# A gated delta-rule layer on one core: whole-row transfers around the substitution, two z buffers, 48 stationary columns in the 16x16 merges, q's squares added on VectorE, new queue orders

## The chip, the core and the metric

The kernel runs on one core of a Trainium2 chip, everything in float32. The metric is the device time of one launch in microseconds. The core has five engines with their own instruction queues (TensorE, VectorE, ScalarE, GpSimd and SyncE, which here only issues DMAs), and they meet only through semaphores.

## What is computed

x has 16 sequences of 256 tokens and 256 channels. The reference is a gated delta-rule attention between layer norms, then a gated feed-forward layer, each added to x. Cut to what matters here (q, k, v, z come from a projection of the normed x, q, k, v through a causal convolution of four taps over time, 32 heads of 64 columns):

```python
q = _l2norm(q) * DK ** (-0.5)
k = _l2norm(k)
def step(Sstate, xs):
    q_t, k_t, v_t, g_t, b_t = xs
    Sstate = Sstate * jnp.exp(g_t)[..., None, None]
    kv = jnp.einsum('bhk,bhkv->bhv', k_t, Sstate)
    delta = (v_t - kv) * b_t[..., None]
    Sstate = Sstate + k_t[..., :, None] * delta[..., None, :]
    o_t = jnp.einsum('bhk,bhkv->bhv', q_t, Sstate)
    return (Sstate, o_t)
_, o = lax.scan(step, S0, (qs, ks_, vs, gs, bs))
var = jnp.mean(o * o, -1, keepdims=True)
o = o * lax.rsqrt(var + EPS) * norm_weight * jax.nn.sigmoid(z)
return o.reshape(Bsz, Sl, VDIM) @ w_out.T
```

## The kernel before

It has three stages. Stage one norms x, turns it and computes the gates for all tokens (8 blocks of 512 tokens). Stage two is the attention. Stage three is the feed-forward layer. The change is in stage two, with a little at the end of stage one.

**Stage two** has 64 steps: 8 groups of four heads times 8 blocks of 512 tokens (two sequences). All is unrolled. The scan is computed in chunks of C = 64 tokens: a step has G = 16 matrices of 64x64 (2 head pairs, 2 sequences, 4 chunks) on each half of the 128 partitions, since two heads share the partitions.

A step passes these stations. `project` (L1142) makes eight 128x512 products of the weights and x: k (0, 1), q (2, 3), v (4, 5), z (6, 7). The taps of the convolution are added: for k and v by VectorE (`conv`, L945), for q by ScalarE (`tap_product`) and GpSimd (`add_tap`). `k_tokens` and `v_tokens` (L1148) turn k and v through a 64x64 identity. `scores` (L1165) makes k'k and q'k, and `matrices` (L992) multiplies them with the decays into `a_mat` (strictly lower triangular once masked) and `p_t`.

Then (1 + A) must be inverted for each chunk. Its four diagonal 16x16 blocks are inverted by forward substitution on VectorE (`substitute`, L958), with 128 blocks side by side, one in each partition. So the blocks travel: `units_out` (L593) writes the diagonal blocks of `a_mat` to `a_d` in DRAM with 8 DMAs, `units_in` reads them with one block per partition, and the inverse goes back two ways: as `x_un` through `x_d` into `x_row`, and turned (`turn_units`) as `t_un` through `z_d` into `z_t` and, its odd blocks, into `z_low`. TensorE then merges pairs of 16x16 blocks (`join16_inner`, `join16_outer`, L1176 to L1192) and pairs of 32x32 blocks (`join_inner`, `join_outer`), with ScalarE copying each product out of bank 5. The scratch tensors hold only the blocks, packed.

Then the chunks run one after the other: `key_state` (old state times k), `residual` (VectorE), `solve` (with z_t), `delta_out` (ScalarE), `advance`, `new_state` (VectorE), `output`. At the end the outputs are normed: var(o) + an epsilon that depends on q's norm. `square_o` squares o into `u_sq`, `square_q` squares q into `q_sq`; `epsilon_q` and `sum_squares` (L1257 to L1261) add both over the 64 rows of a head with two matmuls on the constant matrices `ones[:,1]` and `ones[:,0]` into the same bank. `log_var`, `combine`, `gates`, `gated` follow, then `project_out` and `accumulate` into `acc`.

**The order** is written out by hand. Each engine has a function `turn(s)`, called 67 times; `s[k]` is the step that is k turns old, so one turn carries parts of up to four steps, and every engine executes its list strictly in that order. `wait_for(engine, semaphore, step, ...)` stands ahead of an item that needs another engine's result. SyncE's list (L630) does the same for the DMAs, all on one queue. `mats_done`, `z_in`, `z_low_in`, `x_row_in`, `zt_done`, `rhs_done` are such semaphores.

Four buffers of TensorE's results (banks 0 to 3) are handed round between projections, tokens, scores, squares and output products; bank 4 holds states and solves, bank 5 the merges, banks 6 and 7 the outputs.

## Time and profile before

| | |
|---|---|
| median of 3 runs | 3640.7 us (3633.98 to 3648.48) |
| the profiled execution | 3642.9 us, span 3641.1 us, mean granted TensorE clock 0.974 |
| stage one, two, three | about 0 to 163, 163 to 3251, 3251 to 3641 us |
| busy: TensorE, its weight loads, VectorE, ScalarE, GpSimd | 93%, 63%, 63%, 49%, 30% |
| DMA queue of SyncE | 572208 packets, 267 MB, 27% of 16 engines |

Each float32 matmul shows as two records, with a weight load (PEld) and a matmul (PE) for each. Matmuls are pipelined, so the printed durations of neighbours overlap; the distance between starts is what an item costs in a full queue. "Idle before" an instruction, and who released it, tell whether an engine was waiting. An engine that sits idle while another is full costs nothing.

### The profile page before, as it was taken

To read this page: it belongs to the slowest core of one execution; us is meant where nothing else is said; L and a number is where in the kernel's file an instruction comes from. 1 tells how busy PE (TensorE), PEld (TensorE's weight loads), DVE (VectorE), ACT (ScalarE), POOL (GpSimd) and SP (SyncE) were. 2 spreads that over 40 slices of the span, in tenths; PEclk is the share of its full clock that TensorE was granted. 3 is DMA by queue.
4 is the path that set the end of the run, shared out by engine and by line. 5 is a ranking of instruction groups with operands and counts; after the bars stand their busy time and mean duration, and the time that the engine had idled before them with its cause. 6 is when DMAs were issued, how large, how long until landed. Compare 5 with 4: busy or idle time off the path is not lost. (4 is left out here: it accounts for less than half of the span.)

```text
span 3641.1 us, 118760 instructions
## 1 busy us (share of the span) xinstructions
PE 3372.2 (93%) x51264; PEld 2286.7 (63%) x51264; DVE 2288.9 (63%) x5697; ACT 1788.2 (49%) x3338; POOL 1089.7 (30%) x904
## 2 busy tenths in 40 slices
PE   4489999999999999999999999999999999969998
PEld 2256666666666666666666666666666666645554
DVE  5456666666666666666666666666666666635555
ACT  2245555555555555555555555555555555523333
POOL 1043333333333333333333333333333333300000
PEclk7689999999999999999999999999999999979999
DMA  2233233323333333333332233333332333210000
GB/s 76 65 85 82 82 84 87 83 71 83 85 83 84 87 87 86 86 82 81 85 86 76 77 84 86 85 83 86 87 85 78 84 86 87 63 59 18 23 24 18
DMA packets 572727, 274.83 MB, mean 75 GB/s; under 512 B 475696, under 2 KB 521136, under 8 KB 563888
## 3 DMA queue, kind: packets, MB, share of 16 engines
q1 hardware_dynamic: 572208, 267.25, 27.2%
q8 instruction: 407, 6.67, 0.8%
q14 instruction: 112, 0.92, 0.1%
HBM read 190.02 MB, written 35.13 MB: 62 GB/s over the span
## 5 line engine op out<-in xcount | busy, mean ns | idle before, releaser
L1144 PE MATMUL bank<-xT,w_sb 128*128 128x512 f32 x2048 | 1002.6, 618 | 25.7 <-DMA w_sb<-in_w_qkvz 24.7
L681 POOL TENSOR_TENSOR kq<-kq,products 128x510 f32<-128x510 f32 (+2 forms) x384 | 442.3, 1159 | 892.6 <-ACT products L768 738.4
L1144 PEld LDWEIGHTS bank<-xT,w_sb 128*128 128x128 f32 x2048 | 354.5, 190 | 338.3 <-issue 282.7
L818 ACT COPY delta<-bank 128x256 f32<-128x256 f32 x256 | 95.3, 372 | 639.3 <-PE bank L1227 639.3
L950 DVE SCALAR_TENSOR_TENSOR kq<-bank,cw,kq 128x510 f32<-128x510 f32 (+2 forms) x384 | 285.9, 745 | 101.9 <-ACT kq L762 92.8
L669 POOL TENSOR_TENSOR dec_a<-gcrow,gccol 128x1024 f32<-128x1024 f32 x64 | 121.7, 1901 | 614.0 <-DVE p_t L996 323.5
L950 DVE SCALAR_TENSOR_TENSOR v_c<-bank,cw,v_c 128x510 f32<-128x510 f32 (+2 forms) x384 | 285.8, 744 | 15.2 <-ACT v_c L762 6.2
L1028 DVE TENSOR_TENSOR acc<-acc,bank 128x512 f32<-128x512 f32 x128 | 88.1, 688 | 316.7 <-PE bank L1266 316.7
L1171 PE MATMUL bank<-kq 64*64 64x128 f32 x4096 | 278.5, 275 | 1.7 <-DVE p_t L996 1.7
L1171 PEld LDWEIGHTS bank<-kq 64*64 64x64 f32 x4096 | 217.4, 132 | 76.4 <-issue 71.2
L1266 PE MATMUL bank<-wo,u_sq 128*128 128x256 f32 x1024 | 259.3, 397 | 3.4 <-DVE u_sq L1021 3.4
L768 ACT ACTIVATE products<-bank,cw 128x512 f32<-128x512 f32 x384 | 250.4, 689 | 2.4 <-POOL kq L681 2.4
L1252 PEld LDWEIGHTS bank<-p_t,delta 64*64 64x64 f32 x4096 | 215.1, 136 | 47.8 <-issue 47.8
L1252 PE MATMUL bank<-p_t,delta 64*64 64x64 f32 x4096 | 243.3, 220 | 0.0
L1250 PEld LDWEIGHTS bank<-q_g,state 64*64 64x64 f32 x3072 | 179.6, 134 | 95.5 <-issue 95.5
L968 DVE TENSOR_TENSOR x_un<-x_un,prod_un 128x15 f32<-128x15 f32 (+7 forms) x960 | 200.0, 208 | 32.8
L1266 PEld LDWEIGHTS bank<-wo,u_sq 128*128 128x128 f32 x1024 | 187.1, 192 | 46.8 <-issue 21.3
L964 DVE TENSOR_TENSOR prod_un<-a_un,x_un 128x15 f32<-128x15 f32 (+7 forms) x960 | 196.5, 205 | 26.5
L762 ACT ACTIVATE kq<-bank,cw 128x512 f32<-128x512 f32 x256 | 170.1, 697 | 84.4 <-PE bank L1144 83.2
L1250 PE MATMUL bank<-q_g,state 64*64 64x64 f32 x3072 | 205.9, 226 | 1.1 <-ACT delta L818 1.1
L1227 PE MATMUL bank<-rhs,z_t 64*64 64x64 f32 x3072 | 129.0, 220 | 73.2 <-DVE rhs L1004 73.0
L701 POOL TENSOR_TENSOR dec_a<-dec_a,cols 128x1024 f32<-128x1024 f32 x64 | 121.7, 1901 | 233.0 <-DVE b_eg L990 233.0
(137 smaller groups left out, 6259.7 us busy)
## 6 DMA issues: line engine op xcount, KB each, us to landing
w_sb<-in_w_qkvz SPq DMA_DIRECT2D x64, 1024.0 KB, 6.6
gcrow<-gcrow_d SPq DMA_DIRECT2D x128, 256.0 KB, 4.3
xT<-xT_d SPq DMA_DIRECT2D x64, 512.0 KB, 3.4
k_old<-kq SPq DMA_DIRECT2D x64, 512.0 KB, 3.0
wo<-in_w_out SPq DMA_DIRECT2D x64, 256.0 KB, 6.9
gcrow<-in_x SPq DMA_DIRECT2D x16, 512.0 KB, 3.9
x_un<-eye_un SPq DMA_DIRECT2D x64, 128.0 KB, 2.8
a_d<-a_mat SPq DMA_DIRECT2D x512, 16.0 KB, 1.7
```

Source lines behind the costliest of these rows:

```text
L681: ins = nc.gpsimd.tensor_tensor(t[:, :, d:SEQ], t[:, :, d:SEQ], prod[:, :, 0:SEQ - d], ALU.add)
L762: ins = nc.scalar.activation(dst, bank[:, :], ACT.Identity, scale=cw[:, s * TAPS + TAPS - 1:s * TAPS + TAPS])
L768: ins = nc.scalar.activation(products[i % 4][:, :], bank[:, :], ACT.Identity, scale=cw[:, w:w + 1])
L950: ins = nc.vector.scalar_tensor_tensor(t[:, :, d:SEQ], src[:, :, 0:SEQ - d], cw[:, w:w + 1], t[:, :, d:SEQ], ALU.mult, ALU.add)
L964: own.need(own.mark(nc.vector.tensor_tensor(prod, a_un[:, j + 1:B, j:j + 1].broadcast_to([P, rows, wid]), x_un[:, j:j + 1, 0:wid].broadcas ...
L968: ins = nc.vector.tensor_tensor(rest, rest, prod, ALU.subtract)
L1144: ins = nc.tensor.matmul(bank[:, :], w_sb[:, h, s * P:(s + 1) * P], xT[:, h, :], start=(h == 0), stop=(h == HT - 1))
L1171: ins = nc.tensor.matmul(bank[half, i * P:(i + 1) * P], kq[m.par][half, 0, s // 2, t0:t0 + C], kq[m.par][half, :, s // 2, t0:t0 + C], star ...
L1227: ins = nc.tensor.matmul(banks[4][half, 256 + i * C:256 + (i + 1) * C], z_t[half, g, :], rhs[half, i, :] if c else v_r[m.par][half, g, :], ...
L1250: nc.tensor.matmul(o, state[c % 2][half, i, :], q_g[m.par][half, g, :], start=True, stop=False)
L1252: ins = nc.tensor.matmul(o, delta[half, i, :], p_t[m.par][half, g, :], start=(c == 0), stop=True)
L1266: ins = nc.tensor.matmul(bank[:, t * HID:(t + 1) * HID], u_sq[:, a, (2 * k + t) * P:(2 * k + t + 1) * P], wo[m.par][:, a, :], start=(a == ...
```

## The change

**Layout.** The three scratch tensors become whole 64x64 matrices, each padded by 64 elements, so that a diagonal 16x16 block starts every 16*65 elements. `whole` addresses all rows, `diagonal` only the 16x16 blocks on the diagonal. The zeros off the diagonal of z_d and x_d are written once, at the end of stage one. `z_low` is gone: its blocks are read out of z_t, which has two buffers now. Each transfer is split by partition half: 12 DMAs per step where there were 27.

**The 16x16 merges** load 48 stationary columns instead of 64 (the last 16 rows of the result are not needed) and write 48 rows of bank 5, which is cleared once.

**q's squares** are scaled while they are squared (0.064 squared is 64 x 64 x 1e-6) and added to u's squares on VectorE, so one matmul per half is left.

**The orders** of all five queues are new. TensorE's list is shown whole, of the others the parts around the substitution.

```diff
-        a_d, z_d, x_d = (scratch(n, [UNITS, B, B]) for n in ("a_d", "z_d", "x_d"))
+        a_d, z_d, x_d = (scratch(n, [2, G * MAT]) for n in ("a_d", "z_d", "x_d"))
+        def whole(t, h):
+            return t[h].rearrange("(g x) -> g x", x=MAT)[:, 0:C * C].rearrange("g (i c) -> i g c", c=C)
+        def diagonal(t, h):
+            return t[h].rearrange("(u x) -> u x", x=MAT * B // C)[:, 0:B * C].rearrange("u (i c) -> u i c", c=C)[:, :, 0:B]
...
+                    for h in range(2):
+                        zero = z_t[0][D * h:D * h + D, :, :]
+                        sp.dma_start(whole(z_d, h), zero).then_inc(zeros_out, 16)
+                        sp.dma_start(whole(x_d, h), zero).then_inc(zeros_out, 16)
+                    sp.wait_ge(zeros_out, 64)
...
                     def units_out(m):
                         for h in range(2):
-                            for k in range(4):
-                                u, r = (4 * h + k) * G, D * h + B * k
-                                sp.dma_start(a_d[u:u + G].rearrange("g i j -> i g j"),
-                                             a_mat[m.par][r:r + B, :, B * k:B * k + B]).then_inc(a_d_out, 16)
+                            sp.dma_start(whole(a_d, h), a_mat[m.par][D * h:D * h + D, :, :]) \
+                                .then_inc(a_d_out, 16)
                     def units_in(m):
-                        sp.dma_start(a_un[:, :, :], a_d).then_inc(a_un_in, 16)
+                        for h in range(2):
+                            sp.dma_start(a_un[D * h:D * h + D, :, :], diagonal(a_d, h)) \
+                                .then_inc(a_un_in, 16)
                     def z_out(m):
-                        sp.dma_start(z_d, t_un[:, :, :]).then_inc(z_d_out, 16)
+                        for h in range(2):
+                            sp.dma_start(diagonal(z_d, h), t_un[D * h:D * h + D, :, :]) \
+                                .then_inc(z_d_out, 16)
...
+                            sp.dma_start(z_t[m.par][D * h:D * h + D, :, :], whole(z_d, h)).then_inc(z_in, 16)
...
                     def turn(s):
+                        if s[3]:
+                            identity_in(s[3])
+                        if s[2]:
+                            wait_for(sp, conv_done[5], s[2], 1, back=1)
+                            wait_for(sp, tap_done[5], s[2], 1, back=1)
+                            load_cw(s[2])
+                        if s[3]:
+                            wait_for(sp, mats_done[0], s[3], 1)
+                            units_out(s[3])
                         if s[2]:
                             wait_for(sp, qg_done[1], s[2], 1, back=1)
                             load_gates(s[2])
                         if s[3]:
+                            wait_for(sp, a_d_out, s[3], 32)
                             units_in(s[3])
                             wait_for(sp, zt_done, s[3], 1)
                             z_out(s[3])
+                            load_wo(s[3])
+                            keep_k(s[3])
+                            x_out(s[3])
+                            wait_for(sp, z_d_out, s[3], 32)
+                            z_back(s[3])
+                            wait_for(sp, x_d_out, s[3], 32)
                             x_back(s[3])
+                        if s[1]:
+                            wait_for(sp, proj_full[7], s[1], 1, back=1)
+                            load_xw(s[1])
...
                     def square_q(m):
-                        nc.scalar.activation(q_sq[:, :, :], kq[m.par][:, 1, :, :], ACT.Square)
+                        nc.scalar.activation(q_sq[:, :, :], kq[m.par][:, 1, :, :], ACT.Square, scale=0.064)
...
+                    def add_squares(m, a):
+                        nc.vector.tensor_tensor(u_sq[:, a, :], u_sq[:, a, :], q_sq[:, a, :], ALU.add).then_inc(sq_added[a], 1)
...
                     def join16_inner(m):
-                                ins = nc.tensor.matmul(banks[5][half, g * W2:(g + 1) * W2], a_mat[m.par][half, g, :],
-                                                       z_low[half, g, :], start=True, stop=True)
+                                ins = nc.tensor.matmul(banks[5][D * h:D * h + 3 * B, g * W2:(g + 1) * W2], a_mat[m.par][half, g, 0:3 * B],
+                                                       z_t[m.par][half, g, :].rearrange("p (k e c) -> p e k c", k=2, c=B)[:, 1, :, :], start=True, stop=True)
...
                     def join16_outer(m):
-                                ins = nc.tensor.matmul(banks[5][half, g * W2:(g + 1) * W2], x_row[half, g, :],
+                                ins = nc.tensor.matmul(banks[5][D * h:D * h + 3 * B, g * W2:(g + 1) * W2], x_row[half, g, 0:3 * B],
...
-                    def epsilon_q(m, a, bank):
-                        nc.tensor.matmul(bank[:, :], ones[:, 1, :], q_sq[:, a, :], start=True, stop=False)
-
                     def sum_squares(m, a, bank):
-                        nc.tensor.matmul(bank[:, :], ones[:, 0, :], u_sq[:, a, :], start=False, stop=True).then_inc(ss_full[a], 1)
+                        nc.tensor.matmul(bank[:, :], ones[:, 0, :], u_sq[:, a, :], start=True, stop=True).then_inc(ss_full[a], 1)
```

TensorE's new list for one turn, in words, with the bank and the step's age (1, 2, 3 for s[1], s[2], s[3]; 0 for s[0]), and in brackets what it waits for from VectorE, ScalarE, GpSimd or a DMA:

project 6 (1); output 0 (3); solve 1 (3) [rhs_done 1]; project 2 (1) [conv of k 1]; advance 1 (3) [delta 1]; project 0 (1); output 1 (3); key_state 2 (3) [state 1]; project 3 (1); k_tokens 1 (1) [z_exp 0]; solve 2 (3) [rhs_done 2]; project 4 (1) [tap_done 2]; advance 2 (3) [delta 2]; k_tokens 0 (1) [conv of k 0]; output 2 (3); key_state 3 (3) [state 2]; project 5 (1) [tap_prod 5]; solve 3 (3) [rhs_done 3]; project 7 (1) [kt_done 1]; output 3 (3) [delta 3]; scores 3 (1) [conv 4, tap_added 5]; join16_inner (2) [z_in]; scores 2 (1) [kt_done 0]; scores 1 (1) [conv 5]; join16_outer (2) [p16_done, x_row_in]; scores 0 (1) [z_exp 1]; sum_squares 1 and 0 (3) [sq_added]; join_inner (2) [z16_done]; v_tokens 1 and 0 (1) [mats_done 1, 0]; join_outer (2) [p1_done, xtop_done]; project 1 (0) [comb_done 1, xw_in]; solve 0 (2) [zoff_done]; project_out 1 (3) [og_done]; advance 0 (2) [delta 0]; project_out 0 (3); key_state 1 (2) [k_old_in, state 0].

VectorE's new list: tail (1); substitute columns 2 to 5 (2); new_state 1 (3); substitute columns 6 to 14 (2); residual 2 and decay_state 2 (3); conv 0 (1); new_state 2 (3); sum_k 1, scale_k 1 (1); residual 3 (3); sum_k 0, conv 4, scale_k 0, columns, conv 5, matrices 2 and 3 (1); add_squares 1 and 0 (3); matrices 1 and 0 (1); turn_back (2); combine 1 and 0 (3); scale_v 1 and 0 (1); gated 1 and 0 (3); conv 1 (0); accumulate 1 (3); new_state 0, decay_state 1 (2); accumulate 0 (3); residual 1 (2); substitute columns 0 and 1 (1) [a_un_in, x_un_in].

## Rows read from the trace of the kernel before

**Rows 1.** Busy time by engine, 500 to 3000 us; first line names the columns.
```profile
core 0: us, PE busy (x) PEld busy (x) DVE busy (x) ACT busy (x) POOL busy (x), PEclk, DMA share, GB/s
500.00:3000.00 2500.00, 2420.99 (x41095) 1677.82 (x41095) 1648.60 (x4112) 1337.78 (x2484) 894.38 (x742) 1.00 0.31 84
```
**Rows 2.** TensorE's waits, 500 to 3000 us: total us, times, longest.
```profile
PE bank L1227 <- DVE rhs L1004: 57.2, 54, 1.1
PE bank L1181 <- DMA z_low<-z_d: 11.5, 19, 1.6
PE bank L1144 <- DMA w_sb<-in_w_qkvz: 7.6, 19, 0.7
```
**Rows 3.** Line L1014, the state copy of each step: duration ns, first and last start.
```profile
L1014 DVE COPY state<-bank x64: 424/425/426, 246.0 to 3221.0; 128x256 f32<-128x256 f32 x64
```
**Rows 4.** TensorE's timeline, one turn: start us, duration us, engine, line, operation.
```profile
1500.71 2.06 PE L1181 MATMUL bank<-z_low,a_mat 64*64 64x32 f32 x64
1502.60 2.06 PE L1153 MATMUL bank<-masks,kq 64*64 64x64 f32 x64
1504.49 2.01 PE L1190 MATMUL bank<-p,x_row 64*64 64x32 f32 x64
1506.43 1.98 PE L1144 MATMUL bank<-xT,w_sb 128*128 128x512 f32 x4
1508.34 1.09 PE L1171 MATMUL bank<-kq 64*64 64x128 f32 x16
1509.36 1.20 PE L1199 MATMUL bank<-z_t,a_mat 32*32 32x32 f32 x64
1510.49 1.09 PE L1171 MATMUL bank<-kq 64*64 64x128 f32 x16
...
1526.48 0.63 PE L1227 MATMUL bank<-rhs,z_t 64*64 64x64 f32 x16
1526.94 1.10 PE L1153 MATMUL bank<-masks,v_c 64*64 64x64 f32 x32
...
1533.04 3.70 PE L1144 MATMUL bank<-xT,w_sb 128*128 128x512 f32 x8
1536.67 0.68 PE L1217 MATMUL bank<-state,k_old 64*64 64x64 f32 x16
...
1543.83 1.98 PE L1258 MATMUL bank<-q_sq,ones 128*128 128x512 f32 x4
1545.65 1.88 PE L1261 MATMUL bank<-u_sq,ones 128*128 128x512 f32 x4
1547.46 2.06 PE L1181 MATMUL bank<-z_low,a_mat 64*64 64x32 f32 x64
```
**Rows 5.** DMAs: SyncE's timeline; line L235; issues with KB each, us to landing.
```profile
1519.50 4.17 SPq L597 DMA_DIRECT2D a_d<-a_mat  x8
...
L235 SPq DMA_DIRECT2D gccol_d<-v_r x8: 354/359/367, 38.6 to 157.8; - x8
...
w_sb<-in_w_qkvz SPq DMA_DIRECT2D x64, 1024.0 KB, 6.6
gccol_d<-v_r SPq DMA_DIRECT2D x8, 64.0 KB, 2.1
```
**Rows 6.** Groups of instructions by line: busy us, mean ns, idle before and releaser.
```profile
L950 DVE SCALAR_TENSOR_TENSOR kq<-bank,cw,kq 128x510 f32<-128x510 f32 (+2 forms) x384 | 285.9, 745 | 101.9 <-ACT kq L762 92.8
L968 DVE TENSOR_TENSOR x_un<-x_un,prod_un 128x15 f32<-128x15 f32 (+7 forms) x960 | 200.0, 208 | 32.8
L964 DVE TENSOR_TENSOR prod_un<-a_un,x_un 128x15 f32<-128x15 f32 (+7 forms) x960 | 196.5, 205 | 26.5
L1004 DVE TENSOR_TENSOR rhs<-v_r,rhs 128x256 f32<-128x256 f32 x192 | 119.3, 622 | 6.5
L1021 DVE TENSOR_TENSOR u_sq<-bank,gate 128x512 f32<-128x512 f32 x128 | 87.7, 687 | 80.8 <-ACT gate L829 80.7
L808 ACT COPY p<-bank 32x512 f32<-32x512 f32 x128 | 73.6, 575 | 98.7 <-PE bank L1199 98.0
```

More of the change, by code:

```diff
@@ L44, in gated_delta_sandwich @@
     W2 = 2 * B
-    UNITS = 4 * 2 * G
+    MAT = C * C + C
     TAPS = 4
@@ L95, in gated_delta_sandwich @@
         kt = [sb(f"kt{i}", [P, G, C]) for i in range(2)]
-        z_t = sb("z_t", [P, G, C])
+        z_t = [sb(f"z_t{i}", [P, G, C]) for i in range(2)]
         k_tok = sb("k_tok", [P, G, C])
@@ L116, in gated_delta_sandwich @@
         x_row = sb("x_row", [P, G, C])
-        z_low = sb("z_low", [P, G, W2])
         p16 = sb("p16", [P, G, W2])
@@ L263, in _ @@
                 def _(pool):
-                    nc.gpsimd.memset(z_t[:, :, :], 0.0)
-                    nc.gpsimd.memset(z_low[:, :, :], 0.0)
-                    nc.gpsimd.memset(x_row[:, :, :], 0.0)
+                    nc.gpsimd.memset(z_t[0][:, :, :], 0.0).then_inc(zeros, 1)
                     nc.gpsimd.memset(acc[:, :, :], 0.0)
@@ L1272, in turn @@
                         if s[1]:
-                            wait_for(pe, comb_done[0], s[1], 1, back=2)
-                            project(s[1], 7, banks[0])
-                            wait_for(pe, tap_added[5], s[1], 1)
-                            scores(s[1], 2, banks[1])
+                            wait_for(pe, vr_done[0], s[1], 1, back=1)
+                            project(s[1], 6, banks[0])
+                        if s[3]:
+                            output(s[3], 0)
+                            wait_for(pe, rhs_done[1], s[3], 1)
+                            solve(s[3], 1)
@@ new lines, in turn @@
+                        if s[1]:
+                            wait_for(pe, conv_done[1], s[1], 1)
+                            wait_for(pe, tap_done[1], s[1], 1)
+                            project(s[1], 2, banks[1])
+                        if s[3]:
+                            wait_for(pe, delta_done[1], s[3], 1)
+                            advance(s[3], 1)
+                        if s[1]:
+                            project(s[1], 0, banks[2])
+                        if s[3]:
+                            wait_for(pe, qg_done[1], s[3], 1)
+                            output(s[3], 1)
+                            wait_for(pe, state_done[1], s[3], 1)
+                            key_state(s[3], 2)
@@ new lines, in turn @@
+                        if s[1]:
+                            project(s[1], 3, banks[3])
+                            wait_for(pe, z_exp[0], s[1], 1)
+                            k_tokens(s[1], 1, banks[0])
+                        if s[3]:
+                            wait_for(pe, rhs_done[2], s[3], 1)
+                            solve(s[3], 2)
+                        if s[1]:
+                            wait_for(pe, tap_done[2], s[1], 1)
+                            project(s[1], 4, banks[1])
@@ new lines, in turn @@
+                        if s[3]:
+                            wait_for(pe, delta_done[2], s[3], 1)
+                            advance(s[3], 2)
+                        if s[1]:
+                            wait_for(pe, conv_done[0], s[1], 1)
+                            wait_for(pe, tap_done[0], s[1], 1)
+                            k_tokens(s[1], 0, banks[2])
+                        if s[3]:
+                            output(s[3], 2)
+                            wait_for(pe, state_done[2], s[3], 1)
+                            key_state(s[3], 3)
@@ new lines, in turn @@
+                        if s[1]:
+                            wait_for(pe, tap_prod[5], s[1], 1)
+                            project(s[1], 5, banks[3])
+                        if s[3]:
+                            wait_for(pe, rhs_done[3], s[3], 1)
+                            solve(s[3], 3)
+                        if s[1]:
+                            wait_for(pe, kt_done[1], s[1], 1)
+                            project(s[1], 7, banks[0])
+                        if s[3]:
+                            wait_for(pe, delta_done[3], s[3], 1)
+                            output(s[3], 3)
```

537 lines of the change are left out of this document (224 added, 313 removed).

## Prediction

> **What bounds the kernel now.** I read four views in this order. First the busy time by engine over the middle of the kernel [rows 1]: in 2500 us of the long stage, TensorE is busy for 2421 us (97%) at full granted clock, VectorE for 66%, ScalarE 54%, GpSimd 36%, the DMA engines 31%. So TensorE's queue is the first suspect, but a busy TensorE may hide waits, so next the waits [rows 2]: in the same stretch TensorE waited 57.2 us for `rhs`, 11.5 us for `z_low` and 7.6 us for the projection weights, 76 us in all, and for nothing else worth a number. Third, the pace: the copy that each of the 64 steps makes once [rows 3] starts at 246.0 us and for the last time at 3221.0 us, so 63 turns take 2975 us, 47.22 us each; 2500 us are 52.9 turns, so the waits are 1.44 us of a turn and 45.78 us is TensorE's own work, one instruction behind the other. Fourth, the order of that work in one turn [rows 4], where the distance from one start to the next is what an item costs (the printed durations overlap).
>
> The conclusion: in the long stage (about 3090 of 3641 us) time is the sum of what TensorE executes per turn plus 1.44 us. Removing TensorE work pays in full as long as no other queue comes late.
>
> **The change, part by part (per turn; 63 turns).**
>
> 1. q's squares leave TensorE. Before, two 128x512 matmuls with `ones[:,1]` (four records) stand in one run with the two for u's squares: 1543.83 to 1547.46, 3.63 us for eight records [rows 4]. What stays is four records of that shape alone, which is what a single projection costs: 1506.43 to 1508.34, 1.91 us [rows 4]. Saved: 1.72 us.
>
> 2. The 16x16 merges load 48 stationary columns where they loaded 64. They cost 1.89 us (1500.71 to 1502.60) and 1.94 us (1504.49 to 1506.43) for 64 records, 29.5 to 30.3 ns each. The token transposes with 64 moving columns cost the same 1.89 us as the merge with 32 moving columns [rows 4], so the moving side doesn't set this price. The 32x32 merges, 64 records as well, cost 1.13 us (1509.36 to 1510.49), 17.7 ns a record. The stationary side is the candidate, so 48 columns lie halfway: 1.51 and 1.54 us. Saved: 0.38 + 0.40 = 0.78 us. Bounds: 0 if the price goes by the 64x64 tile and not by its columns, and 1.57 us if it falls right to 1.13. I take the middle because the tile size doesn't change, only the columns. That the moving operand is now read in two groups of 16 columns from z_t I cost at nothing, since the moving side isn't the limit.
>
> The Trainium skill has a rule that speaks against this part: "TensorE: Matmul & The Clock Gate", section "Wait — 56ns, not 53.3ns?", says that start-to-start never falls below about 25 ns however small a matmul is. By it the two merges would cost 64 x 25 = 1.60 us each and save 0.63 us (an estimate from that page), 9 us of the whole less. The trace disagrees for this kernel, with 17.7 ns a record in the 32x32 merges.
>
> 3. The new order of TensorE. Two projections in a row cost 3.63 us (1533.04 to 1536.67), one alone 1.91 [rows 4]: each further run of full-array work costs about 0.19 us. Before there are 10 runs in a turn; in the new order 11 (projections 6, 2, 0, 3, 4, 5, 7, the squares, projection 1, and each output projection alone). Added: 0.19 us.
>
> TensorE's own work comes to 45.78 - 1.72 - 0.78 + 0.19 = 43.47 us per turn (42.7 to 44.25 by the bounds of 2).
>
> 4. VectorE adds q's squares: two all-SBUF 128x512 additions. No such form is in the trace; the nearest is the 128x512 product with one PSUM operand, 0.69 us [rows 6], so 1.4 us, with no gain possible since nothing is taken off VectorE. It stands after two `matrices` and ahead of `sum_squares` by a merge and a score product (1.5 + 1.02 us of TensorE), and VectorE goes from 66% of 47.2 us (31.2 us) to 32.6 of 43.5 (75%). Hidden. If GpSimd works beside it, the stretch seen on the all-SBUF `residual` (0.62 us mean [rows 6], against 0.42 for a copy of the same size [rows 3]) would make it some 2 us.
>
> 5. The `rhs` wait. Before, `key_state` and the `solve` behind it stand next to each other, so each turn pays residual's latency; this is the 1.08 us wait of every turn [rows 2]. In the new order each `key_state` is followed by at least a projection and a transpose, or by a projection, or (across the turn's end) by a projection and an `output`: 1.91 us or more, against two residual operations, 0.62 us for the all-SBUF one [rows 6] and 0.42 for the one from PSUM, taken like the state copy [rows 3]. The wait goes. What is late next? I walked the new queues with the rows' durations. VectorE starts a turn with residual 1 (1.04), the substitution (15 columns, (200.0+196.5+32.8+26.5)/64 = 7.1 us [rows 6]) and a state, so it reaches residual 2 at about 9.5 to 10 us and ends it at 11. TensorE wants it when it has done four projections (7.64), one half of the key transposes (0.95) and some 3 us of chunk products (0.46 for 16 records [rows 4]): at 11.6 us. Slack 0.6 us. Then come a decay (0.42) and a convolution of k (3 x 0.745 [rows 6]), over at 13.7 us; the second half of the transposes wants it after one more projection and two chunk products, at 14.4: slack 0.7 us. ScalarE's evacuation of the first 32x32 product (2 x 0.575 us [rows 6]) has 1.9 us of transposes to hide behind: slack 0.7 us. All positive and none large, so I take 0.2 us of waits per turn, not 0.
>
> 6. Transfers of whole rows. `units_out` was 8 issues taking 4.17 us, 256 pieces of 64 bytes each [rows 5]; it becomes 2 issues of 1024 pieces of 256 bytes. The way in, and z and x on the way out, were contiguous and become 1024 pieces of 64 bytes each in 2 issues. In all 27 issues become 12, and the pieces rise from about 6,500 to 12,300. Stage one has a transfer of exactly this shape, `gccol_d`, 1024 pieces of 64 bytes: 0.36 us to issue, 2.1 us to land [rows 5]. At that price a hop costs about 0.7 + 2.1 us. Upper bound: issue time by the piece, 4.17/2048 = 2.0 ns, so 4.2 us for each pair. z_t must be back for `join16_inner`. The substitution ends at about 10 us of the turn; TensorE reaches the merge after four more projections, both transposes, six chunk products and a score product, at about 23 to 24 us. Chain: turning the blocks 0.6 (taken like ScalarE's 0.575 [rows 6]), z_out 0.7, the w_out and k copies 0.8, x_out 0.7, z_back 0.7, landing 2.1: 5.6 us, so at about 16 us, 18 with some queueing. With 4.2 us for each of the three pairs it is 16 us, so z lands at 26 and TensorE waits 2 us. I take the first since it is a measured transfer of this very shape. The `z_low` wait (0.22 us per turn) goes. The weight load now waits for projection 7 and stands behind x_back; it lands 6.6 us after its issue, and until `project(s[0],1)` TensorE has some 14 us: the 0.14 us of weight waits go too. Queued behind the load are only the identity copy and the next `units_out`, which waits for the matrices 10 us later.
>
> 7. Once: zeros to z_d and x_d, four transfers of 256 KB at the end of stage one, which the next stage waits for: 4 issues and a landing, less what overlaps, +3 us (0 to 8). Filling and draining: a step's life grows from about 2.7 to 3.2 turns, but the last turns are emptier and shorter. I take 0 (-14 to +14).
>
> **Sum.** 43.47 + 0.2 = 43.67 us per turn, 3.55 us less than 47.22. Times 63: -223.7 us; +3: -221. Against the profiled execution (3642.9 us, its span 3641.1) that gives 3422; the median of the runs is 2 us lower, so 3420 us.
>
> **Rivals.**
>
> A. Waits come back elsewhere. The slacks of 5 are under 1 us, and where GpSimd works beside VectorE an SBUF operation is half as long again. One late residual or convolution per turn would restore 1 to 2 us: 3470 to 3535, about 3495. For it: the kernel already had 1.44. Against: no queue is over 75% busy and the waits before had one plain cause.
>
> B. 48 columns cost what 64 cost. Then only 0.78 us is missing: +49, 3469 us.
>
> C. Slower than before: z comes back too late. TensorE's queue is in order, so the wait at `join16_inner` stops everything. The gain of 3.55 us is eaten once z lands over 3.5 us after 23.5, at 27 us of the turn, 9 to 11 us later than I have it. With the issue cost by the piece (26 us) and the pieces moving at half the pace, 5 us late would be +1.5 us per turn, 3735 us. For it: the pieces double, and z and x are now written in 64-byte pieces with gaps between them. Against: `gccol_d` does the same in 2.1 us, and the DMA engines are 31% busy.
> The Trainium skill, "DMA: Bandwidth & Descriptors", section "Specifications", says that below 512 bytes a transfer does read-modify-write and leaves line rate, which speaks for C; no row here shows the cost per piece for more than 1024 pieces at once.
>
> D. Better than forecast: the merges fall to 1.13 us or the draining is shorter: 3360 to 3385.
>
> **Chances.** Forecast (3385 to 3445) 0.58, A 0.20, B 0.10, C 0.05, D 0.07. The range 3385 to 3510 takes in the forecast, B and two thirds of A: 0.81. Within 0.5% (3622 to 3659; about what a measurement of this kernel can tell from no change) only a mix of A and C ends: 0.01. Faster 0.94, slower 0.05.
>
> **What would show it.** The state copies 43.7 us apart; no `ones` matmul but the one for u's squares; merges of 1.4 to 1.6 us from start to start; no `rhs` wait on `solve`; z_back landing by 18 us of the turn. It is wrong if TensorE shows waits over 0.5 us per turn (then their releaser names A or C), or if the merges still take 1.89 us.

## The result and the profile after

The changed kernel takes 3621.8 us (median of 6 runs, 3612.1 to 3636.3) beside 3641.2 us for the kernel before: a ratio of 0.9948 with a 95% interval of 0.9923 to 0.9974. The prediction was 3420 us, with a range of 3385 to 3510, so of the 221 us that it promised 19 arrived. The profiled execution has a span of 3626.6 us. The experiments below win 146 of the missing 202 us: with two short edits the changed kernel runs in 3475.7 us.

The views of the changed kernel are shown in the order in which those of before were read. Its page, part 1 and two lines of part 3 (queue, kind: packets, MB, share of 16 engines):

```profile
PE 3284.2 (91%) x51008; PEld 2221.8 (61%) x51008; DVE 2486.1 (69%) x5826; ACT 1769.1 (49%) x3338; POOL 1093.2 (30%) x902
...
q1 hardware_dynamic: 929648, 343.73, 40.3%
q8 instruction: 406, 6.65, 0.8%
```

The middle of the kernel by engine, with the columns of [rows 1]:

```profile
500.00:3000.00 2500.00, 2363.01 (x41249) 1636.67 (x41247) 1830.45 (x4263) 1334.00 (x2508) 911.57 (x753) 0.99 0.47 110
```

TensorE was busy for 2421 of these 2500 us before and is busy for 2363 now. It does less and stands more. The state copy of each step [rows 3]:

```profile
L1000 DVE COPY state<-bank x64: 414/417/425, 251.9 to 3204.5; 128x256 f32<-128x256 f32 x64
```

63 turns take 2952.6 us, 46.87 each where there were 47.22 and 43.67 were forecast. That is nearly the whole miss: 3.20 us x 63 is 202 us of the 206 by which the profiled execution (3628.4 us) missed its forecast of 3422. The rest is what stands outside the 63 turns, 8 us where 3 were forecast (the first copy 5.9 us later, what follows the last copy 2.0 us longer). TensorE's waits in the same stretch, against [rows 2]:

```profile
PE bank L1219 <- DVE rhs L988: 54.2, 53, 1.0
PE bank L1182 <- issue: 48.2, 34, 3.0
PE bank L1200 <- issue: 19.8, 26, 1.6
PE bank L1162 <- issue: 7.8, 6, 1.9
```

Two things stand here that the forecast had at 0.2 us together. The `rhs` wait is as large as before, 54.2 us or 1.02 us a turn. Below it are waits that name no releaser ("issue": the engine waited for nothing that the profile shows), at the inner and outer merges and the score products, 82 us with the smaller rows of the view, 1.54 us a turn; before they were 1.9 us in the whole stretch. The merge waits for nothing that another engine does. What does it wait for?

**A stop, looked at closely.** TensorE's timeline around one of them (start, duration, then as in [rows 4]):

```profile
1542.42 1.59 PE L1173 MATMUL bank<-z_t,a_mat 64*48 64x32 f32 x63
...
1543.90 1.94 PE L1162 MATMUL bank<-kq 64*64 64x128 f32 x31
1545.62 0.51 PE L1182 MATMUL bank<-p,x_row 64*48 64x32 f32 x15
1548.47 1.77 PE L1182 MATMUL bank<-p,x_row 64*48 64x32 f32 x49 [2.34 <-issue]
```

The stop is inside one loop of 64 matmuls, after the 15th, where no instruction waits on a semaphore. The DMA queues in the 9 us up to it, and in the 1.3 us behind them:

```profile
q1 hardware_dynamic: 4492, 2.10, 90.6%
```

```profile
q1 hardware_dynamic: 121, 0.48, 93.0%
q8 instruction: 1, 0.02, 5.1%
```

The page names q8 the instruction queue. It moved 6.65 MB in 406 packets, 16.4 KB each. TensorE has 51008 matmuls and as many weight loads, and with the 1989 records of its sequencer (the part that waits and branches) 104,005 instructions in the trace, 256 for each packet, so this queue is the supply of TensorE's instructions. Between 1536.9 and 1545.9 us it moved nothing, at 1546.01 one packet, and TensorE goes on at 1548.47. The stretch from `scores` 3 to `join_outer` is nearly all small matmuls, some 400 of them with a weight load each: three packets' worth in about 17 us.

Is the packet late, or is TensorE simply too fast for it? Count TensorE's records in the trace up to each packet's start. In the kernel before, packet by packet between 500 and 3000 us, TensorE is then 23 records short of a multiple of 256 (median). The packet at 1546.01 starts when TensorE is 193 records past one, which it had passed at 1542.78 us, and the 62 packets behind a stop of over 0.5 us start 94 past (median). So they are late against TensorE's own progress. From 60 records short of the multiple until such a packet starts, the DMA engines' mean busy share was 0.96 (median), and under 0.70 for only 2 of the 62. On SyncE's queue stands what the DMA engines had to do meanwhile:

```profile
1534.85 3.17 SPq L621 DMA_DIRECT2D z_t<-z_d  x2
1539.21 1.29 SPq L630 DMA_DIRECT2D x_row<-x_d  x2
1540.72 0.58 SPq L577 DMA_DIRECT2D xT<-xT_d  x1
1541.35 0.43 SPq L578 DMA_DIRECT2D w_sb<-in_w_qkvz  x1
```

The change put the load of 1 MB of weights behind projection 7, beside the start of the densest stretch of TensorE's list, and the 4096 pieces of z's and x's way back in front of it. The same stretch by windows (columns of [rows 1]; PEclk, DMA share and GB/s are the last three):

```profile
1541.00:1544.00 3.00, 3.00 (x109) 3.00 (x106) 2.35 (x5) 2.42 (x4) 2.49 (x2) 1.00 1.15 257
1544.00:1546.00 2.00, 2.00 (x50) 2.00 (x47) 0.93 (x3) 1.08 (x2) 1.85 (x4) 1.00 0.97 383
1546.00:1548.50 2.50, 0.16 (x8) 0.09 (x5) 2.50 (x6) 0.00 (x0) 0.87 (x1) 1.00 0.67 252
1548.50:1551.00 2.50, 2.50 (x59) 2.50 (x60) 0.18 (x1) 0.70 (x2) 0.00 (x0) 0.60 0.05 15
```

The DMA engines are full while TensorE is still at work, and TensorE stands in the third window. The fourth shows a second price: after the stop the granted clock is 0.60, so most of this window ran at 1.2 GHz instead of 2.4. In 500 to 3000 us the clock record has 65 us at 1.2 GHz in 16 stretches, each right after a stop of 1.6 to 3.0 us; in the kernel before it has none.

**Why the rhs wait stayed.** VectorE's queue ahead of `solve` 2, and GpSimd's at that time:

```profile
1525.52 0.22 DVE L944 TENSOR_TENSOR prod_un<-a_un,x_un 128x55 f32<-128x55 f32 x1
1525.77 1.16 DVE L948 TENSOR_TENSOR x_un<-x_un,prod_un 128x55 f32<-128x55 f32 x1
1526.97 1.12 DVE L944 TENSOR_TENSOR prod_un<-a_un,x_un 128x48 f32<-128x48 f32 x1
1528.13 0.21 DVE L948 TENSOR_TENSOR x_un<-x_un,prod_un 128x48 f32<-128x48 f32 x1
...
1530.03 0.43 DVE L988 TENSOR_TENSOR rhs<-v_r,rhs 128x256 f32<-128x256 f32 x1
```

```profile
1525.53 2.50 POOL L678 TENSOR_TENSOR kq<-kq,products 128x510 f32<-128x510 f32 x2 [10.08 <-ACT kq L752]
```

Two substitution operations of 0.2 us took 1.16 and 1.12 us, each until one of GpSimd's two additions (1.25 us each) was over. So residual 2 starts late, at 1530.03 us, and `solve` at 1530.60 has waited 1.03 us.

### The profile page after: what moved, and what is told of

Read it like the earlier page. It is cut to its first block and busy times, and to the rows that moved or that the text cites. A ratio compares the mean times of both kernels' runs of the same rounds, so it can differ in the third digit from the quotient of the medians.

```text
span 3626.6 us, 117234 instructions
## 1 busy us (share of the span) xinstructions
PE 3284.2 (91%) x51008; PEld 2221.8 (61%) x51008; DVE 2486.1 (69%) x5826; ACT 1769.1 (49%) x3338; POOL 1093.2 (30%) x902
## 3 DMA queue, kind: packets, MB, share of 16 engines
q8 instruction: 406, 6.65, 0.8%
## 5 line engine op out<-in xcount | busy, mean ns | idle before, releaser
L1134 PE MATMUL bank<-xT,w_sb 128*128 128x512 f32 x2048 | 1023.0, 623 | 22.0 <-DMA w_sb<-in_w_qkvz 17.5
L948 DVE TENSOR_TENSOR x_un<-x_un,prod_un 128x15 f32<-128x15 f32 (+7 forms) x960 | 258.1, 269 | 32.9
L944 DVE TENSOR_TENSOR prod_un<-a_un,x_un 128x15 f32<-128x15 f32 (+7 forms) x960 | 255.8, 266 | 29.9 <-DMA a_un<-a_d 3.3
L1162 PEld LDWEIGHTS bank<-kq 64*64 64x64 f32 x4096 | 237.2, 137 | 19.1 <-issue 19.1
L977 DVE TENSOR_TENSOR a_mat<-bank,dec_a 128x256 f32<-128x256 f32 x256 | 106.8, 417 | 173.1 <-PE bank L1162 172.8
L790 ACT ACTIVATE z_t<-bank 16x256 f32<-16x256 f32 x256 | 95.8, 374 | 204.8 <-PE bank L1182 202.5
```

Of the source, the lines that this page charges most:

```text
L944: own.need(own.mark(nc.vector.tensor_tensor(prod, a_un[:, j + 1:B, j:j + 1].broadcast_to([P, rows, wid]), x_un[:, j:j + 1, 0:wid].broadcas ...
L948: ins = nc.vector.tensor_tensor(rest, rest, prod, ALU.subtract)
L1134: ins = nc.tensor.matmul(bank[:, :], w_sb[:, h, s * P:(s + 1) * P], xT[:, h, :], start=(h == 0), stop=(h == HT - 1))
L1162: ins = nc.tensor.matmul(bank[half, i * P:(i + 1) * P], kq[m.par][half, 0, s // 2, t0:t0 + C], kq[m.par][half, :, s // 2, t0:t0 + C], star ...
```

## Experiments

The theories: **supply**, that TensorE runs out of instructions because the packet that brings them queues behind data on full DMA engines (and loses clock afterwards); against it **volume**, that the added pieces or their landing are the cost wherever they stand, and **pace**, that the small matmuls outrun any fetch, whatever the DMA engines do; and **GpSimd**, that its additions beside the substitution make the `rhs` wait. Each run is given with its median, its ratio to the kernel before with interval, and the pace of its state copies. The table at the end sets all of them side by side.

### The weight load, once in eight steps

The weights of eight steps are the same 1 MB; here the other seven loads move 16 pieces of 64 bytes, in the same place of the queue.

```diff
-                        sp.dma_start(w_sb[:, :, :].rearrange("p h t -> p (h t)"), w_qkvz[m.index() // NSP]) \
-                            .then_inc(xw_in, 16)
+                        if m.index() % NSP == 0:
+                            sp.dma_start(w_sb[:, :, :].rearrange("p h t -> p (h t)"), w_qkvz[m.index() // NSP]) \
+                                .then_inc(xw_in, 16)
+                        else:
+                            sp.dma_start(w_sb[0:16, 0, 0:16], w_qkvz[m.index() // NSP][0:16, 0:16]).then_inc(xw_in, 16)
```

> The changed kernel, but the 1 MB projection weights are loaded only in the first of the 8 steps that use them; in the other 7 a piece of 16 x 64 bytes of the same data is loaded in their place. Theory F: TensorE's mid-item stops in the dense stretch of small matmuls (80 us of waits without a releaser in 500 to 3000 us, 1.5 us per turn, each ending about 2.4 us after a 16 KB instruction packet starts) are its own instruction fetches, held up behind the weight load that the new order places in that stretch. Then these waits fall below 0.3 us per turn and the kernel takes 3490 to 3530 us instead of 3622. Rival S: the small pieces of the a, x and z transfers hold up the fetch; then the waits stay above 1 us per turn and the time within 15 us of 3622. Rival D: the stretch simply consumes instructions faster than they are fetched; the same as S in time, with the stops where they were.

Measured: 3552.7 us, 0.9754 (0.9731 to 0.9777), 45.70 us a turn. The unnamed waits fall from 1.54 to 0.93 us a turn, the time at 1.2 GHz from 65 to 10 us; the `rhs` wait stays at 1.01. The theory was written too strongly: it expected stops under 0.3 us and 3490 to 3530 us, so this load is a part of the cause and not the whole. No wait in the trace of the changed kernel pointed at this load in the middle of the kernel, and taking it away is worth 69 us. The control is the same edit in the kernel before, where the load stood elsewhere:

> The kernel before with the weights loaded once in 8 steps: a control for the first experiment (3553 for 3622 us, -69). In the kernel before the load stands beside projections and TensorE shows no unreleased waits (0.03 us per turn), so F expects only the small z_low and weight waits to go (0.36 us per turn): 3620 to 3640 us. If a 1 MB load costs TensorE time wherever it stands: 3570 to 3590 us.

Measured: 3642.5 us, 0.9987 (0.9977 to 0.9996), 3 to 5 us, just short of the 3620 to 3640 expected: the wait for the weights is gone, but those for `rhs` and `z_low` grew from 57.2 to 60.0 and from 11.5 to 13.7 us. So in the old orders the load costs next to nothing; the 69 us are a price of the new ones.

### GpSimd's addition after the substitution

One wait is added on GpSimd, so that the additions of q's taps start when the substitution is over.

```diff
                             wait_for(pool, tap_done[2], s[3], 1)
+                            wait_for(pool, sub_done[5], s[3], 1, back=1)
                             add_tap(s[3], 0, 1)
```

> The changed kernel, but GpSimd's first tap addition of a step waits until the substitution of the step before is over. Theory G: VectorE's all-SBUF operations stand still while a GpSimd addition runs (0.68 and 1.16 us instead of 0.20 and 0.21 for the substitution operations that meet one, 1.9 us per turn in all), and this is what makes residual 2 late by 1.03 us in each turn. Then the rhs wait of solve goes below 0.1 us per turn and the kernel takes 3550 to 3570 us. Rival: the tap additions, 4 us later, make the second half of q late in turn; then scores or project 5 wait and the time stays within 15 us of 3622 or above it.

Measured: 3569.7 us, 0.9793 (0.9775 to 0.9810), 46.01 us a turn. The `rhs` wait is gone from TensorE's waits:

```profile
PE bank L1183 <- issue: 40.5, 22, 2.5
PE bank L1201 <- issue: 13.3, 19, 1.7
PE bank L1145 <- DVE kq L931: 13.0, 54, 0.2
```

and the substitution's operations are back at the duration of [rows 6] (the first line is the changed kernel's, the second this run's):

```profile
L948 DVE TENSOR_TENSOR x_un<-x_un,prod_un 128x15 f32<-128x15 f32 (+7 forms) x960 | 258.1, 269 | 32.9
```

```profile
L949 DVE TENSOR_TENSOR x_un<-x_un,prod_un 128x15 f32<-128x15 f32 (+7 forms) x960 | 198.6, 207 | 32.9
```

What is late next is the key transposes' wait for a convolution of k, 0.24 us a turn. The unnamed waits stay in the main (1.27 us), so the `rhs` wait has a cause of its own.

### 64 columns again in both 16x16 merges

```diff
-... banks[5][D * h:D * h + 3 * B, g * W2:(g + 1) * W2], a_mat[m.par][half, g, 0:3 * B], ...
+... banks[5][half, g * W2:(g + 1) * W2], a_mat[m.par][half, g, :], ...
```

and the same for `x_row` in `join16_outer`.

> The changed kernel with 64 stationary columns in both 16x16 merges again. If time is the sum of TensorE's items, 64 records at 29.5 ns for 23.5 in two merges give +0.8 us per turn: 3670 us. If the stops for instructions take what slower items give back, because the records of the merges are what drains the instruction buffer, less: 3625 to 3645 us, with the unreleased waits falling from 1.5 us per turn to under 1.

Measured: 3626.8 us, 0.9948 (0.9933 to 0.9963), 46.93 us a turn. The merge does take longer, 1506.37 to 1508.21 where the changed kernel has 1542.42 to 1543.84:

```profile
1506.37 2.05 PE L1173 MATMUL bank<-z_t,a_mat 64*64 64x32 f32 x64
1508.21 1.99 PE L1162 MATMUL bank<-kq 64*64 64x128 f32 x32
```

The time moves by 5 us only (0 by the ratios), because the unnamed waits fall from 1.54 to 1.04 us and the time at 1.2 GHz from 65 to 41 us. This fits that a slower merge uses up instructions more slowly: what the 48 columns save, TensorE stands waiting for its next instructions or loses in clock. Without the stops the same edit has its full price (below).

### q's squares back on TensorE

```diff
-nc.tensor.matmul(bank[:, :], ones[:, 0, :], u_sq[:, a, :], start=True, stop=True).then_inc(ss_full[a], 1)
+nc.tensor.matmul(bank[:, :], ones[:, 1, :], q_sq[:, a, :], start=True, stop=False)
+nc.tensor.matmul(bank[:, :], ones[:, 0, :], u_sq[:, a, :], start=False, stop=True).then_inc(ss_full[a], 1)
```

VectorE's addition becomes a copy of one column, and the square has no scale, as before the change.

> The changed kernel with q's squares summed by a second matmul on TensorE again, and the two additions on VectorE replaced by one-column copies. If removing the matmuls was worth what they cost, 1.7 us per turn comes back: 3729 us. If TensorE's time there was partly cover for instruction fetches: 3670 to 3700 us. If VectorE's additions cost more than the matmuls did, 3622 us or less.

Measured: 3760.9 us, 1.0312 (1.0294 to 1.0329), 49.10 us a turn, 2.23 more than the changed kernel; 0.36 of it are more stops and some 0.3 more time at the low clock. That is above all three values that were expected. The four records that come back to a turn bring more stops, where the wide merges brought fewer; the runs don't show why.

### The pieces taken away

From the third step on, the transfers of a, z and x are cut down; instructions and waits are the same.

```diff
-                            sp.dma_start(z_t[m.par][D * h:D * h + D, :, :], whole(z_d, h)).then_inc(z_in, 16)
+                            if m.index() < 2:
+                                sp.dma_start(z_t[m.par][D * h:D * h + D, :, :], whole(z_d, h)).then_inc(z_in, 16)
+                            else:
+                                sp.dma_start(z_t[m.par][D * h:D * h + 16, 0, 0:16], whole(z_d, h)[0:16, 0, 0:16]).then_inc(z_in, 16)
```

and so for the other five. This version leaves work out: from the third step on its inverses are stale.

> The changed kernel, but from the third step on each of the a, x and z transfers moves only 16 pieces of 64 bytes in place of 1024 (so the inverses are stale and the output isn't the reference's); weights are loaded in every step. It takes away 12,000 small pieces per turn and leaves the order of all engines. If DMA traffic of any kind holds up TensorE's instruction fetch (F with the pieces as the larger part), the unreleased waits fall from 1.5 to under 0.5 us per turn: 3510 to 3550 us. If only the 1 MB weight load does (it took 0.6 of the 1.5 us in the first experiment): within 15 us of 3622. If the small matmuls outrun any fetch (D): the waits stay above 0.9.

Measured: 3607.0 us, 0.9887 (0.9848 to 0.9925), 46.45 us a turn, stops 1.33. Stops and low clock together stay at 2.09 us where they were 2.15; of the 0.42 us won, 0.35 are own work. With the weight load reduced as well:

> As the kernel without the small pieces, and the weights loaded only once in 8 steps. DMA share then falls well under that of the kernel before. F: no unreleased waits above 0.1 us per turn, 3450 to 3500 us (what is left is the rhs wait of 1.0 us per turn). D: 0.9 us per turn of unreleased waits stay, as in the first experiment, and the time is within 20 us of its 3553.

Measured: 3499.1 us, 0.9602 (0.9578 to 0.9627), 44.73 us a turn, stops 0.25. By the ratios, taking away the 12,300 pieces of a turn is worth 0.6% (22 us), the weight load 1.9% (71 us), both 3.5% (126 us), more than the two together (the pieces' share is barely clear of the intervals): they have one victim, and the load by itself is enough to keep it waiting. This speaks against volume, which had the pieces as the main part, and against pace: with the same list of instructions the stops fall to 0.25 us once the transfers are gone.

### Both edits together

> The two edits that helped together: weights once in 8 steps and GpSimd's taps after the substitution. If their causes are separate the gains add: 3622 - 69 - 52 = 3500 us (3490 to 3515). If the second only moves waiting from one place to another (TensorE's buffer refills while it waits for rhs), less: 3520 to 3545 us.

Measured: 3475.7 us (3472.3 to 3477.7), 0.9532 (0.9516 to 0.9548), 44.50 us a turn. Its waits and its state copy:

```profile
PE bank L1148 <- DVE kq L934: 13.5, 56, 0.2
PE bank L1204 <- issue: 10.1, 16, 1.1
PE bank L1186 <- issue: 7.5, 5, 2.2
```

```profile
L1004 DVE COPY state<-bank x64: 415/418/425, 252.7 to 3056.3; 128x256 f32<-128x256 f32 x64
```

It leaves no work out and is the fastest version, 166 us under the kernel before and 146 under the changed one (169 and 152 by the ratios). Added up, the two edits alone would give 3500 us; it is 24 us less, outside the 3490 to 3515 that were expected of separate causes. With the load reduced, the later additions take away not only 0.77 us of named waits (1.01 to 0.24) but also 0.56 us of stops (0.93 to 0.37). So the two causes are not wholly separate; what links them was not tested.

### The same megabyte in two places

This sets place against volume. To the version above a spare transfer of 1 MB from DRAM to DRAM is added in every step, once in the sparse part of TensorE's list (behind `units_in`), once in the dense part (behind `load_xw`, where the weight load had been).

```diff
                             units_in(s[3])
+                            load_spare(s[3])
```

> The combined kernel (weights once in 8 steps, taps later; 3476 us) with a spare 1 MB copy inside DRAM in each step, issued right behind units_in, so beside the projections and chunk products of the turn's first half. If what matters is the place of the traffic against TensorE's dense stretch (F), it costs little: 3476 to 3500 us, unreleased waits under 0.6 us per turn. If what matters is how much is moved: 3540 us and more.

```diff
                             load_xw(s[1])
+                        if s[2]:
+                            load_spare(s[2])
```

> The same spare 1 MB copy, issued behind the loads that follow projection 7, where the changed kernel has its weight load: beside the merges, scores and token transposes. F: the stops come back (over 1 us per turn, and stretches at half clock with them): 3550 us and more. Volume: the same as with the copy in the first half.

Measured: 3478.7 us, 0.9546 (0.9532 to 0.9560) in the sparse place; 3576.3 us, 0.9791 (0.9751 to 0.9830; runs from 3549.7 to 3584.4) in the dense one. The middle of each, sparse first, and its waits:

```profile
500.00:3000.00 2500.00, 2458.39 (x43342) 1708.89 (x43338) 1970.76 (x4489) 1410.28 (x2638) 955.77 (x788) 1.00 0.51 117
```

```profile
PE bank L1157 <- DVE kq L943: 13.4, 56, 0.2
PE bank L1213 <- issue: 12.1, 18, 1.2
PE bank L1195 <- issue: 7.0, 6, 1.9
```

```profile
500.00:3000.00 2500.00, 2403.09 (x41659) 1657.47 (x41659) 1888.87 (x4319) 1356.65 (x2537) 917.48 (x755) 0.98 0.49 114
```

```profile
PE bank L1214 <- issue: 27.0, 25, 3.3
PE bank L1196 <- issue: 25.6, 11, 3.9
PE bank L1176 <- issue: 15.7, 9, 3.7
```

The same bytes cost 3 to 5 us in one place (by the medians and by the ratios) and 98 us more in the other (89 by the ratios), although the sparse one has the higher DMA share (0.51) and rate (117 GB/s). No engine that computes waits for the spare tile. The mean share of the DMA engines doesn't tell the two apart; what counts is where the transfer stands against the stretch in which TensorE uses its instructions fastest.

### The two TensorE edits priced without the stops

64 columns in the version with both edits:

> The combined kernel (3476 us) with 64 stationary columns in the 16x16 merges. In the changed kernel 64 columns cost only 5 us more than 48. If the stops for instructions had swallowed the gain, it shows here where they are 0.4 us per turn instead of 1.5: (29.5 - 23.3) ns x 128 records = 0.79 us per turn, 3525 us (3505 to 3530). If 48 columns are worth nothing anywhere: 3470 to 3485 us.

Measured: 3524.6 us, 0.9673 (0.9659 to 0.9688), 45.23 us a turn, 0.73 more than the version it is made from and 49 us in all. This is what was expected of it (3505 to 3530). With the stops the same edit had cost 0 to 5 us. q's squares back on TensorE in the same version:

> The combined kernel (3476 us) with q's squares summed on TensorE again and VectorE's two additions replaced by one-column copies. The term of the forecast is 1.72 us per turn: 3584 us (3570 to 3600). In the changed kernel the same edit cost 139 us, 2.2 us per turn; if that excess came from more stops and more time at the low clock, it is gone here.

Measured: 3624.2 us, 0.9947 (0.9932 to 0.9961), 46.81 us a turn, 2.31 more. The expectation (3570 to 3600) was wrong: the excess over 1.72 us did not go with the load and the late taps. 0.42 us of it are stops and 0.13 low clock.

### All runs side by side

Per turn, from three views of each profile: the pace of the state copies; the unnamed waits and the named waits of TensorE between 500 and 3000 us; half of the time at 1.2 GHz in that stretch (what ran at half clock is counted as having taken twice as long, an estimate); and what is left, TensorE's own work.

| run | pace | stops | named waits | low clock | own work |
|---|---|---|---|---|---|
| before | 47.22 | 0.03 | 1.44 | 0 | 45.75 |
| changed | 46.87 | 1.54 | 1.02 | 0.61 | 43.70 |
| before, weights once | 47.23 | 0.02 | 1.39 | 0.03 | 45.79 |
| weights once | 45.70 | 0.93 | 1.01 | 0.09 | 43.67 |
| taps later | 46.01 | 1.27 | 0.24 | 0.66 | 43.84 |
| 64 columns | 46.93 | 1.04 | 1.03 | 0.38 | 44.48 |
| q's squares back | 49.10 | 1.90 | 1.02 | 0.90 | 45.28 |
| pieces gone | 46.45 | 1.33 | 1.01 | 0.76 | 43.35 |
| pieces and weights gone | 44.73 | 0.25 | 1.01 | 0.06 | 43.41 |
| weights once, taps later | 44.50 | 0.37 | 0.24 | 0.09 | 43.80 |
| + spare, sparse place | 44.53 | 0.38 | 0.24 | 0.06 | 43.85 |
| + spare, dense place | 46.24 | 1.42 | 0.24 | 0.76 | 43.82 |
| + 64 columns | 45.23 | 0.31 | 0.24 | 0.03 | 44.65 |
| + q's squares back | 46.81 | 0.79 | 0.24 | 0.22 | 45.56 |

Eight of these runs have the changed kernel's TensorE list with its 48 columns and one sum of squares; their own work is 43.35 to 43.85 us, while their paces differ by 2.4 us. What differs is how long the list stands.

## Why the prediction was wrong

**The sum of the work held.** 43.47 us a turn was forecast for TensorE's own work, the table has 43.70, in a bound of 42.7 to 44.25. Of the parts:

- Part 1, q's squares, 1.72 us: the difference of own work is 1.58 us with the stops and 1.76 without (45.56 less 43.80). Right for own work, but low for what the edit is worth: the paces differ by 2.23 and 2.31 us, since the extra records also bring more stops and low clock.
- Part 2, the merges, 0.78 us: own work differs by 0.78 and 0.85 us. Right, and rival B (48 columns cost what 64 cost) falls. From start to start the merge takes 1.42 to 1.48 us for 64 records, 23 ns each, which is again under the about 25 ns that the Trainium skill gives as the least in "TensorE: Matmul & The Clock Gate", section "Wait — 56ns, not 53.3ns?".
- Part 4, VectorE's additions: forecast 0.7 us each, 2 us a pair beside GpSimd. Measured, 829 ns each (busy, mean):

```profile
L1020 DVE TENSOR_TENSOR u_sq<-u_sq,q_sq 128x512 f32<-128x512 f32 x128 | 101.2, 829 | 12.0 <-ACT u_sq L809 12.0
```

  TensorE waited for them once in the whole kernel, 1.4 us. Hidden, as forecast.
- Some 0.2 to 0.3 us of own work stand over the forecast of 43.47, and in the two runs with the pieces gone they don't (43.35 and 43.41). This points to stops too short for the view of waits, but wasn't settled.
- Part 7: what is paid once, with filling and draining, came to 8 us where 3 were forecast. The two parts of it can't be told apart here.

**The first step that failed** is the sentence that removing TensorE work pays in full as long as no other queue comes late. The queue that came late, the instruction supply, was in none of the views that the argument was built on, though the page lists it in part 3 as 0.8% of the engines. Its price is 1.54 us of stops and 0.61 us of low clock a turn, 2.15 x 63 = 135 us, of which reducing the weight load brings back 1.13 us a turn. It sits in part 6: of the weight load only its landing (6.6 us) was set against the 14 us until its user, and "queued behind the load are only the identity copy and the next `units_out`" looked at SyncE's queue alone. On the DMA engines the next instruction packet is queued behind it too. Of what the change does, two things are shown to make this worse: the place of the largest transfer of the turn beside the small matmuls, and the narrower merges (0.50 us of stops and 0.23 of low clock, 0.12 together in the version with both edits). Taking out the squares made it better. That the small matmuls stand closer together was not varied by itself.

**The second** is part 5: slack 0.6 us for residual 2 was worked out with the substitution at its duration of before, 7.1 us. GpSimd's additions of q's taps now overlap it, and VectorE loses 1.83 us a turn there (its 30 operations take 8.03 us, and 6.20 with the additions later), more than the slack; the wait stayed at 1.02 us. The stretch beside GpSimd was in the text, for the residual and for the additions of part 4, but not for 30 small operations whose mean of 0.2 us showed no trace of it; before, an addition of GpSimd touched only 30 of the 1920, starting within 0.1 us of them, and 29 took no longer. Its price is 0.78 us a turn of named waits, 49 us (1.02 less 0.24 with the additions later); the pace falls by 0.86. The Trainium skill states the mechanism in "SBUF — State Buffer", section "SBUF: two separate sides": VectorE and GpSimd share a pair of ports, and when a VectorE operation with two SBUF inputs meets a GpSimd operation that reads SBUF, the second one to start is blocked until the first is over. The 1.16 and 1.12 us above agree. By that rule the order of GpSimd's queue against the substitution would have been the thing to walk.

**Mis-sized, but hidden:** the transfers of part 6. `gccol_d` (0.36 us to issue, 2.1 to land [rows 5]) was the wrong neighbour, since it runs alone. The page's part 6 has:

```profile
w_sb<-in_w_qkvz SPq DMA_DIRECT2D x64, 1024.0 KB, 7.9
...
a_d<-a_mat SPq DMA_DIRECT2D x128, 256.0 KB, 3.9
...
z_t<-z_d SPq DMA_DIRECT2D x128, 256.0 KB, 4.6
x_row<-x_d SPq DMA_DIRECT2D x128, 256.0 KB, 4.5
```

and the pair of z_t takes 3.17 us to issue (shown above), near the upper bound of 4.2 by the piece. In the turn shown, z is back at about 1541.5 us (its second half was issued at 1537.3, and 4.1 us is the shortest time to landing of this line) and `join16_inner` starts at 1542.42: one microsecond to spare where the text had five to eight. Rival C was that near; in the whole kernel TensorE waited for z once, 1.2 us.

**The rivals.** A (waits come back elsewhere, 3470 to 3535 us) was right in kind, and the `rhs` wait is an instance of it. But its 1 to 2 us were priced by data waits alone, and its times are low for them: 63 and 126 us over 3420 are 3483 to 3546. Named and unnamed waits together with the clock are 3.2 us a turn. No rival had the supply, and so the range was too narrow by 112 us. The sign of being wrong, waits over 0.5 us a turn, came true, but most of them named no releaser, where the text had only A or C to name.

**Added up:** own work 43.70, rhs 1.02, stops 1.54 and low clock 0.61 are 46.87 us. The forecast had 43.47 + 0.2. The difference of 3.20 us is 2.15 for the supply, 0.82 for `rhs` and 0.23 for own work.

**Still open.** That the packet waits behind data on full DMA engines follows from the windows, from the count of records at the packets' starts, from the control and from the spare megabyte in two places. What orders the packets within an engine, and whether a smaller or split load in the same place would let the packet through, wasn't tried. Nor was the weight load moved, with its full size, to the sparse place; the spare transfer there suggests that most of the 69 us would stay. The wide spread of the dense run (35 us) is not explained, nor why q's squares on TensorE bring more stops.

## To carry to other kernels

When TensorE is full, a removed microsecond is only won if its instructions come as fast as it uses them: count the instructions of the densest stretch of small matmuls, look at the page's instruction queue, and keep large loads and thousands of small pieces out of the time just before it. A wait called "issue" inside one unbroken loop, with a packet of that queue some 2 us before its end, is the sign. When a VectorE chain of small SBUF operations is moved, move GpSimd's work out from beside it, and price the chain by what overlaps it in the new order, not by its mean in the old.

## What the runs showed of the hardware

- TensorE's instructions come in packets of 16.4 KB, 256 instructions, on the DMA engines that carry the data. All 78 unnamed waits of TensorE in the changed kernel between 500 and 3000 us ended 2.2 to 5.5 us (median 2.4) after the start of the last such packet.
- After a stop of 1.6 to 3.0 us the granted clock may go to 1.2 GHz: all 16 such stretches of the changed kernel between 500 and 3000 us follow one, 65 us in all, 82 with the spare megabyte in the dense place, 7 with it in the sparse place, none before.
- A matmul with 32 moving columns of float32 costs 23 ns from start to start with 48 stationary columns and 29 ns (1.84 us for 64 records) with 64: here the price went by the stationary side.
- VectorE's operation of 0.2 us took up to 1.2 us beside a GpSimd addition of 1.25 us.
